# A two-layer attention and mixture-of-experts kernel: four edits in the order of work (last norms, rows of z, late roundings, products of constants)

## What is computed

```python
x = x + L0_xattn(_layernorm(x), ctx)            # q + (tril * (ctx ctx^T)) q, no softmax
x = x + L0_ffn(_layernorm(x), w12, w3, gate_w)  # the two best of 8 experts by gate score
x = x + L1_xattn(_layernorm(x), ctx, ctx, mask) # softmax attention, rows masked
x = x + L1_ffn(_layernorm(x), w1, b1, w2, b2)   # rmsnorm, 8-bit activations, ternary weights

def L0_ffn(x, w12, w3, gate_w):
    topk_scores, topk_idx = top_k(x @ gate_w.T, 2); p = softmax(topk_scores)
    h1, h2 = split(x @ w12[e].T); y = sum over the two e of p_e * ((silu(h1) * h2) @ w3[e].T)

def bitlinear(x, w, b):   # L1_ffn: gelu between two of these
    xn = rmsnorm(x); xq = clip(round(xn * 127 / max|xn|), -128, 127) * max|xn| / 127
    return xq @ ternary(w).T + b
```

## Time and profile before

| | before |
|---|---|
| median of 3 runs | 690.27 us (689.24 to 691.34) |
| profiled execution: time, span | 690.07 us, 687.6 us |
| busy: PE, DVE, ACT, POOL | 559.8, 512.2, 359.3, 394.6 us |
| mean granted TensorE clock | 0.881 of 2.4 GHz |

### The profile page before, as it was taken

One profiled execution on the slowest core, in us unless ns is written; L12 is line 12 of the kernel. 1 busy time (PEld: TensorE's weight loads), 2 busy tenths in 40 slices (PEclk: granted clock), 3 DMA queues, 4 the chain that ended last, 5 costly groups with the idle time before them and its releaser, 6 DMA issues.

```text
span 687.6 us, 17582 instructions
## 1 busy us (share of the span) xinstructions
PE 559.8 (81%) x5806; PEld 485.2 (71%) x5806; DVE 512.2 (74%) x1475; ACT 359.3 (52%) x662; POOL 394.6 (57%) x469
## 2 busy tenths in 40 slices
PE   6897961067999899999999999961787667999996
PEld 5776850037999899999999999960655533566664
DVE  6897866756797977666666656535898598999994
ACT  2254667612444344434444443421667947999992
POOL 1064556579999998888886433331002025888753
PEclk9765675569999999999999999995698789999999
DMA  8598994336455223778896755638793300011111
GB/s 305 185 312 291 346 379 148 125 78 154 95 155 136 54 33 48 93 97 96 99 102 81 71 63 64 117 40 289 215 355 101 90 1 1 17 46 40 41 47 62
DMA packets 103165, 87.22 MB, mean 127 GB/s; under 512 B 55075, under 2 KB 94883, under 8 KB 102054
## 3 DMA queue, kind: packets, MB, share of 16 engines
q1 hardware_dynamic: 89782, 68.27, 35.6%
q0 software_dynamic: 13296, 17.83, 16.0%
HBM read 44.35 MB, written 32.41 MB: 112 GB/s over the span
## 4 chain that ended last, share of the span: by engine, by line
PE 56%; DVE 12%; issue 5%; ACT 3%; DMA 2%; SPq 0%; DVEq 0%; ACTq 0%; POOLq 0%
PE banks L1086 27%; PE banks L1099 15%; PE banks L1725 4%; PE banks L1701 3%; PE banks L1704 2%; PE banks L1715 2%; DVE h_rounded L1989 1%; PE banks L1637 1%; DVE hidden_T_low L1192 1%; PE banks L1629 1%; DVE ffn_amax L1962 1%; ACT hidden_ffn L1597 1%; DMA expert_rows_in<-rows_of_tokens 1%; DVE x_rows L1753 1%; PE banks L1723 1%
## 5 line engine op out<-in xcount | busy, mean ns | idle before, releaser
L1086 PE MATMUL banks<-z_turned,w_of_block 128*128 128x128 f16 x3408 | 203.9, 220 | 0.8 <-DMA z_turned<-z_rows 0.5
L1086 PEld LDWEIGHTS banks<-z_turned,w_of_block 128*128 128x128 f16 x3408 | 191.9, 98 | 4.4 <-issue 1.5
L1055 POOL DMA_INDIRECT rows_of_tokens<-x_rows,row_tokens x71 | 122.7, 1728 | 71.7 <-ACT x_rows L1154 46.3
L1186 DVE SCALAR_TENSOR_TENSOR hidden_T<-banks,blk_inv,silu_T 128x512 f32<-128x512 f32 x71 | 53.3, 751 | 84.4 <-PE banks L1086 82.5
L504 POOL DMA_INDIRECT z_rows<-z_parts,places_in_regions x64 | 66.5, 1039 | 76.3 <-DVE z_parts L777 44.1
L1145 ACT ACTIVATE hidden_T_high<-hidden_T 128x512 fp32r<-128x512 f32 x71 | 44.9, 632 | 122.1 <-DVE hidden_T L1186 111.6
L1178 DVE COPY w_of_block<-w_parts 128x4096 f16 x71 | 97.5, 1374 | 8.4 <-DMA z_rows<-z_parts,places_in_regions 4.2
L1099 PE MATMUL banks<-w_low,hidden_T_high 128*128 x284 | 85.8, 302 | 8.5 <-DVE hidden_T_low L1192 8.3
L1138 ACT ACTIVATE silu_T<-banks,blk_inv 128x512 f32<-128x512 f32 x71 | 48.8, 687 | 70.3 <-PE banks L1086 60.4
L1099 PE MATMUL banks<-w_high,hidden_T_high 128*128 x284 | 79.3, 279 | 0.0
L1099 PE MATMUL banks<-w_high,hidden_T_low 128*128 x284 | 79.2, 279 | 0.0
(11 more groups left out here) (268 smaller groups left out, 1239.7 us busy)
## 6 DMA issues: line engine op xcount, KB each, us to landing
w_parts<-in_w SPq DMA_DIRECT2D x7, 1024.0 KB, 9.3
x_rows<-in_x SPq DMA_DIRECT2D x8, 512.0 KB, 6.2
w_parts<-in_ctx_and_x_turned SPq DMA_DIRECT2D x8, 512.0 KB
w_high<-in_ctx_and_x_turned SPq DMA_DIRECT2D x8, 512.0 KB
w_low<-in_w SPq DMA_DIRECT2D x8, 512.0 KB
rows_of_tokens<-x_rows SPq DMA_DIRECT2D x8, 512.0 KB, 3.9
rows_of_tokens<-zero_rows SPq DMA_DIRECT2D x8, 512.0 KB, 3.6
w_last_in<-in_ctx_rows SPq DMA_DIRECT2D x32, 128.0 KB, 3.4
```

The lines of the kernel that those rows point to most:

```text
L1055: pool.indirect_dma_start(token_rows[:, :], bass.IndirectOffsetOnAxis(ap=dest[:, j:j + 1], axis=0), X1[:, j % T, :], None, compute_op=ALU. ...
L1086: mm = pe.matmul(PS[:, 1 + half + 2 * u, hc * P:(hc + 1) * P], win[:, u, wp, c, at:at + P], zturn[:, j % ZB, k, :], start=(n == 0), stop=( ...
L1186: v.scalar_tensor_tensor(out=g[:, :], in0=PS[:, 2 + 2 * u, :], scalar=blk_inv[:, j:j + 1], in1=s[:, :], op0=ALU.mult, op1=ALU.mult).then_i ...
```

## The change

1. `batch_step` loses batch 7; its norms are opened in step 33 (T + 1), after the last tile's moments, so that `links()` issues them in turn with `choose(5)`.
2. `z_step` of tiles 26 to 31 is one lower (steps 34, 34, 35, 35, 36, 36), and the loop has 38 steps.
3. `high_w(0)` and `high_w(1)` leave the steps and stand with `high_w(2)` after the loop; `low_w(0)` comes after the loop ahead of `block_tables`, `low_w(1)` and `low_w(2)` behind it.
4. `turn_p` issues three products of constants (`ident16` times three copies of itself, 384 columns) into the unused columns of its bank, behind the wait for `pt_kept` and ahead of the wait for `p_made`; 96 in all.
5. `round_h` of tiles 28 to 31 stands in steps 33 to 36, each in its own step like the others.

```diff
@@ -357,7 +357,7 @@
 
         batches = ((0, 4, None, None), (4, 8, None, None), (8, 14, 0, 4), (14, 20, 4, 8), (20, 26, 8, 13),
                    (26, 32, 13, 19), (32, 32, 19, 26), (32, 32, 26, 32))
-        batch_step = {1: 1, 2: 6, 3: 10, 4: 15, 5: 21, 6: 28, 7: 34}
+        batch_step = {1: 1, 2: 6, 3: 10, 4: 15, 5: 21, 6: 28}
         spans, col_x, col_z, batch_x, batch_z = [], {}, {}, {}, {}
         n = 0
         for b, (x0, x1, z0, z1) in enumerate(batches):
@@ -373,7 +373,7 @@
         z_step = {t: t + 7 if t < 8 else t + 8 if t < 13 else t + 9 for t in range(19)}
         z_step.update({t: t + 10 for t in range(19, 23)})
         z_step.update({23: 33, 24: 33, 25: 34})
-        z_step.update({26 + n: T + 3 + n // 2 for n in range(6)})
+        z_step.update({26 + n: T + 2 + n // 2 for n in range(6)})
         z_tiles = {s: [t for t in z_step if z_step[t] == s] for s in range(T + 12)}
         ROUTES = ((0, 4), (4, 8), (8, 13), (13, 19), (19, 26), (26, 32))
         route_end = [t1 for t0, t1 in ROUTES]
@@ -383,7 +383,7 @@
             pieces.append(list(zip(cuts[:-1], cuts[1:])))
         pieces_done = [sum(len(p) for p in pieces[:r + 1]) for r in range(len(ROUTES))]
         route_of = {t: r for r, (t0, t1) in enumerate(ROUTES) for t in range(t0, t1)}
-        STEPS = T + 7
+        STEPS = T + 6
         w12_step = {8: 0, 10: 1, 12: 2, 15: 3, 18: 4, 21: 5, 23: 6, 25: 7}
         w3_step = {14: 0, 17: 1, 20: 2, 27: 3, 28: 4, 29: 5, 30: 6, 31: 7}
         square_at = {}
@@ -575,10 +575,7 @@
                         exp_gaps(route_end.index(s - 3))
                     for n in square_at.get(s, ()):
                         square(n)
-                    if s in (T + 2, T + 4):
-                        high_w((s - T) // 2 - 1)
-
-                for e in range(2, PRE):
+                for e in range(PRE):
                     high_w(e)
 
             def pe0(pe):
@@ -953,6 +950,8 @@
                         links()
                     if 2 <= s <= T + 1:
                         x1_moments(s - 2)
+                    if s == T + 1:
+                        norm_links = norms(len(batches) - 1)
                     for _ in range(NORM):
                         links()
                     if s - 2 in route_end:
@@ -963,10 +962,9 @@
                         tell_tails()
                     if s == T + 1:
                         scale()
-                    if s in (T + 3, T + 5):
-                        low_w((s - T) // 2 - 1)
+                low_w(0)
                 block_tables()
-                for e in range(2, PRE):
+                for e in range(1, PRE):
                     low_w(e)
 
     st = ExitStack()
@@ -1640,6 +1638,9 @@
 
                 def turn_p(i, k):
                     after(pe, pt_kept, R * i + k)
+                    for _ in range(3):
+                        pe.matmul(PS[:, 3, P:4 * P], ident16[:, :], ident16[:, :].unsqueeze(1).broadcast_to([P, 3, P]),
+                                  start=True, stop=True)
                     pe.wait_ge(p_made, R * i + (k + 1))
                     pe.transpose(PS[:, 3, 0:P], pr[:, k % Q, :], ident[:, :]).then_inc(pt_made, 1)
 
@@ -2018,15 +2019,13 @@
                     if s + R < T:
                         largest_x(s + R)
                     advance(chain_x, 1)
-                    for t in ([s - 5] if 0 <= s - 5 < T - Q else ()):
+                    for t in ([s - 5] if 0 <= s - 5 < T else ()):
                         round_h(t)
                     advance(normed[3], 2 if s < 12 else NORM_N)
                     advance(chain_x, 1)
                     if 0 <= s - 1 < T:
                         largest_h(s - 1)
                     advance(chain_x, 1)
-                    if s == T:
-                        round_h(T - Q)
                     if s in h_ended:
                         advance(chain_h, L2)
                         chain_h = scale_h(h_ended[s])
@@ -2034,9 +2033,6 @@
                     advance(chain_x, 1)
                     if s in h_ended:
                         advance(chain_h, 1)
-                    if s == T:
-                        for t in range(T - Q + 1, T):
-                            round_h(t)
                     if (s % Q == Q - 1 and s < T - Q) or s == T + 5:
                         advance(chain_h, L2)
                     if 0 <= s - 8 < T:
```

## The result

The changed kernel takes 682.7 us (median of four runs, 681.66 to 685.52) against 690.19 for the kernel before on the same chip: ratio 0.9881, 95% interval 0.9842 to 0.9921, so 7.5 us or 1.1% faster. Both are in the direction forecast; the size lies between 4 and 8 us. The profiled execution is the slowest of the four, 685.52 us with a span of 683.7, so the trace shows 3.9 us of span less and not 7.5.

The account below looks back on a forecast made before the run. It took TensorE to bound the expert stage, a scatter-and-load chain the end of layer 0, and no single engine layer 1's attention. 690.07 - 4.2 - 4.0 + 2.0 = 683.9, on the median's level 684.1 us; range 680.0 to 690.5.

Parts of the forecast that it names:

- signs of being right: GpSimd without idle, tiles 24 to 31; first expert product near 147; tail wait about 1 us; late tiles near 2.0 apart.
- Late roundings, -4.0: Kernel's tail: finish of tile 24 comes sooner, -2.7 us, and the clock's fall behind it goes, -1.3; ends -1.3 and -4.5.
- Norms, z and weights, -4.2: End of layer 0: the first expert product moves from 151.25 to 147.0, -4.2 us; ends -6 and -1.
- If both idles go (2.55 + 2.60), the last scatter is issued at 140.5: End of layer 0: GpSimd loses its idles of 2.55 and 2.60 us; the last scatter has landed by 142.9.
- the weights become the bound: Rival, end of layer 0: weights, one chain of 17.8 us without cover, move the start only 1 us: 687.3; chance 0.17.
- lower end of -6: Best case of the -4.2 us term at the end of layer 0, with scatters also less stretched.
- the gain allowed for low parts behind the last scatter: End of layer 0: low parts after the last scatter cost GpSimd nothing, making the term up to 1 us better.
- Constants, +2.0: Layer 1's attention: +1.6 and +0.9 where TensorE is full, +0.3 at 522 to 528, -0.8 for better clock; bounds +15.4, -1.5.
- the constants hold the clock: Rival, layer 1's attention: clock held at 2.4 GHz, net -1.0 in place of +2.0 us, so 681.1; chance 0.14.
- if the clock is up by then: Layer 1's attention, 522 to 528: the stretch would shorten towards ScalarE's 4.91 us, -1.1, against +1.5; +0.3 was taken.
- they would set the pace: Rival, layer 1's attention: no wait covers the constants, most tiles pay; slower, 693.6 with 24 paying; chance 0.11.
- it moves as a block: Expert stage, 151 to 459 us: nothing of the change is in it, TensorE busy 298.95 of 308 us.

Follow-up runs that it names:

- e3: The kernel before with norms interleaved, z one step earlier and the weights' parts behind z, nothing of layer 1: 687.83 us, ratio 0.9972.
- e9: The kernel before with only the loads of the tokens' table moved behind two turned loads instead of four: 678.97 us, ratio 0.9991.
- e8: The changed kernel with VectorE's nine steps of the weights' scale one step later, behind low z of tiles 23 and 24: 672.77 us, ratio 0.9895.
- e11: The changed kernel with table loads behind two turned loads, weights' scale one step later, no constants for the last seven tiles: 669.18 us, ratio 0.9845.
- e2: The kernel before with only the three products of constants per tile of layer 1's attention added: 688.8 us, ratio 0.9971.
- e6: The changed kernel with six products of constants per tile in place of three: 681.43 us, ratio 1.0014 to the kernel before.
- e7: The changed kernel without products of constants for tiles 25 to 31 of layer 1's attention: 673.79 us, ratio 0.9924 to the kernel before.
- e12: The changed kernel itself, run again on a third chip: 676.23 us, ratio 0.9945 to the kernel before.
- e10: The changed kernel with one product of constants per tile in place of three: 674.13 us, ratio 0.9918 to the kernel before.
- e1: The kernel before with only the roundings of tiles 28 to 31 each in its own step: 686.81 us, ratio 0.9951.

## Why the prediction was right, and where it was not

684.1 us was forecast, in a range from 680.0 to 690.5; 682.7 came. The total is nearer than its terms, and that is luck. Layer 0 gave 1.6 to 3.8 us less than its term and the constants 3.0 more than theirs, which cancels, and the expert stage, in no term, moved by +3 us in one profile and by -3 in another. As a ratio the forecast was 0.991, between the 0.9881 and the 0.9945 that were measured. Of the signs of being right, the first product came at 150.69 and not near 147, the late tiles 1.70 us apart and not near 2.0; only the tail's came as said.

*Late roundings, -4.0.* Right in every step: finish 24 starts at 671.23 (forecast 670.7 to 671.5), the wait is 1.30 (about 1), the 1.89-us group is gone; -4.1 measured.

*Norms, z and weights, -4.2.* The direction was right, the size not: -2.6 in the profile of the change, -0.9 in e3, and on the third chip *choice* is 40.15 and 40.23 against 40.63 in e9, -0.4. The step that failed is "If both idles go (2.55 + 2.60), the last scatter is issued at 140.5": it was issued at 144.12. Both went, but one of 2.89 us came before tile 23, which the term did not price. To have the norms early I had put them, and the scale's nine steps behind them, ahead of low z of tiles 23 and 24. The new idle's size hangs on pauses in those steps: 3.67 us with them here, 3.60 in e3 (idle 2.72), 2.07 without on the other two chips (idle 1.20); where the steps come after low z, it is gone (e8, e11). Why they pause there and not on the others stays open. The estimate of the weights' end was good (forecast 141.8 to 145.8, it was 145.25), and so were the 3.2 us from landing to start (3.14). The rival that the weights become the bound fell: e8 starts earlier still, with the weights done before the last scatter. The lower end of -6 rested on scatters "less stretched": four are, by 0.7 to 1.1 us each and 3.8 in sum, where five were by 4.0, always beside a low part of weights; the last was issued at 144.12, beside the low part begun at 144.04, so the gain allowed for low parts behind the last scatter was not to be had. The Trainium skill's rule that the later of VectorE and GpSimd waits for the shared ports ("SBUF — State Buffer", "Who interferes with whom") agrees with the four stretched ones (an issue of 1.96 us in place of 0.96 beside an operation of 1.21 us). It does not explain the issues at 138.06, 139.32 and 142.86, which began while a low part of w12 ran and took 0.96 us all the same.

*Constants, +2.0.* Wrong in sign: -1.0 by length, and e2's interval (up to 1.0002) leaves no room for +2.0, though it does for nothing at all. The rival "the constants hold the clock" was right in mechanism and in its net of -1.0. Two steps failed. First the price: I took TensorE's busy time as its load, 5.70 of 6 us at 1.54 a tile, so 1.46 a tile, and +0.4 each late tile; the load is 1.22 (e6 against the change), and three constants cost 0.17 there. The late stretch cost some 0.8 us and not 1.6, and 503 to 509 cost nothing and not 0.9 (its 1.71 stayed 1.71). Second, "if the clock is up by then": it was. The three spacings after the tile at 519.04, 4.00, 3.24 and 2.54 us, became 3.42, 3.20 and 1.87, -1.3 where I took +0.3. The rule of the Trainium skill that the throttled clock is the default and activity releases it ("TensorE: Matmul & The Clock Gate", "What's actually happening") fits the trace: 0.50 and 0.54 without, 1.00 and 1.00 with the constants in the profile of the change (0.72 in the first stretch of e7 and e11). That they would set the pace is a matter of number: six do (e6), three nearly, one does not.

*"it moves as a block".* The expert stage did not. That nothing of the change is in it was true, but the step left out that its second block waits for a load whose landing varies by 2.5 us, and that TensorE's clock falls for 0 to 10 us in the stage. In the profile of the change this gave back 3.1 us; in e12's it gave 3 more. No term of the sum had it, in either direction.

## What to carry to other kernels

The busy time of a modelled, pipelined engine is no price list: its load per tile is what the spacing says once that engine alone sets it, and doubling the suspect (three products to six) gives both load and price in one run. When a producer's chain is shortened, list all that stands ahead of the consumer on the same queue, not only what the profile names as the releaser, since the next in line takes the place of what went. To hold TensorE's clock through waits, begin with the least work that does it, and leave it out where tiles follow without a pause.

## What the runs showed of the hardware

- One product of 384 columns per tile (0.16 us) did for the clock in the second stretch where ScalarE is the bound what three did (1.00 for 0.54). In the first the clock fell for 6.8 us in all five profiles without constants, for 3.4 us with one (e10), and with three for 3.4 us in two of seven.
- Behind a wait of 5.88 us TensorE ran 6 us at a clock of 0.50. Behind one of 3.35 us it ran 3.4 us at 0.50 in the kernel before and in e1, and none in e12; e8, with a wait of 1.93 us, had 10.2 us at 0.50. Idle time and half of the time at 0.50 explain the stage's length in all fourteen profiles to within 1.6 us.
- Nine small dependent operations of VectorE took 1.92 us in the kernel before and 3.67 in the changed one, with pauses of 0.49, 1.22 and 0.48 us between them; on two other chips the same order took 2.07.
- Eight loads of 2 KB, issued in 4.11 us behind four turned loads (6.1 to 6.7 us of issues), landed 1.2 to 3.7 us after the last of them; issued behind two, they were there when wanted.
- The time of the kernel before differs by 10 us between chips (690.07 and 679.33). The traces put it before the end of layer 0: the first expert product comes at 150 to 153 us on one and 140 to 145.5 on the others (the changed kernel: 150.69 and 144.01), with the later stages alike.
